# First rows of the expert weights subtracted by eight plain adding DMAs with repeated source rows, in place of sixteen gathers

## The reference

```
xn = _layernorm(x, axis=-1)
x = x + attn(xn) + ffn(xn)
attn: k, v, r = xn @ W.T;  wkv = scan over time of exp-weighted v;  out = (sigmoid(r) * wkv) @ out_w.T
ffn:  scores = softmax(xn @ gate_w.T + gate_b);  top 2 of 8 experts
      expert e: h = silu(xt @ w1e.T + b1e) * (xt @ w3e.T + b3e);  y = h @ w2e.T + b2e
      y = sum over the chosen experts of gate * y_e;  plus one shared expert of width 512
```

## Time and profile before

| | |
|---|---|
| runs of the kernel | 493.45 us median of 3 (492.17 to 494.56) |
| the profiled execution's own time | 489.11 us |
| its span, first to last instruction | 487.4 us |
| PE busy | 435.8 us (89%) |
| POOL busy | 265.7 us (55%) |
| DMA software queue q0 | 8816 packets, 21.93 MB, 17.4% of 16 engines |
| DMA hardware queue q1 | 37388 packets, 55.85 MB, 33.5% of 16 engines |

### The profile page before, as it was taken

The page is one execution under the profiler, slowest core; times in us unless marked ns, Lnnn a source line. Parts: engine busy times, 40 slices in busy tenths (PEclk is TensorE's granted clock), DMA queues, the critical chain, the costliest instruction groups (busy, mean ns, idle before and its releaser), DMA issues.

```text
span 487.4 us, 8291 instructions
## 1 busy us (share of the span) xinstructions
PE 435.8 (89%) x2522; PEld 367.0 (75%) x2522; DVE 382.1 (78%) x707; ACT 227.1 (47%) x365; POOL 265.7 (55%) x237
## 2 busy tenths in 40 slices
PE   0896064989999999999999998999999999999997
PEld 0442053778988889888888776989898989898987
DVE  7896996876788698886966478897887969696953
ACT  1445342675876858678485543141323242414131
POOL 5005988746285865859846587837262645445000
PEclk9999555799999999999999998999999999999999
DMA  5879994326567485342454692352626170705001
GB/s 177 259 253 279 304 236 97 96 80 197 209 228 250 120 270 182 133 169 91 154 144 168 213 346 69 113 200 87 195 76 206 36 244 21 258 2 174 11 33 45
DMA packets 46242, 78.27 MB, mean 161 GB/s; under 512 B 5788, under 2 KB 32132, under 8 KB 46204
## 3 DMA queue, kind: packets, MB, share of 16 engines
q1 hardware_dynamic: 37388, 55.85, 33.5%
q0 software_dynamic: 8816, 21.93, 17.4%
HBM read 49.55 MB, written 28.21 MB: 160 GB/s over the span
## 4 chain that ended last, share of the span: by engine, by line
PE 69%; DVE 8%; POOL 8%; issue 6%; DMA 5%; SPq 1%; ACT 1%; POOLq 0%; DVEq 0%; ACTq 0%
PE ps_g L971 15%; PE ps_y L971 7%; PE ps_w L1429 6%; PE ps_w L1431 5%; PE ps_w L1430 5%; PE ps_w L1495 5%; PE ps_w L1496 5%; PE ps_w L1494 5%; DMA w_lo<-w_all 4%; POOL xg L893 3%; PE ps_x L965 3%; PE ps_h L991 2%; POOL w_lo L367 2%; PE ps_v L1429 1%; PE ps_v L1431 1%
## 5 line engine op out<-in xcount | busy, mean ns | idle before, releaser
L893 POOL DMA_INDIRECT xg<-xn_rows,tile_tok x71 | 72.4, 1020 | 30.0 <-issue 17.1
L1398 POOL DMA_INDIRECT yg<-expert_rows,rows x64 | 66.2, 1034 | 23.6 <-issue 17.1
L971 PE MATMUL ps_g<-w_hi,x_hi 128*128 x142 | 57.3, 404 | 2.3 <-DVE w_lo L380 1.7
L971 PE MATMUL ps_g<-w_lo,x_hi 128*128 x142 | 57.0, 402 | 0.0
L971 PE MATMUL ps_g<-w_hi,x_lo 128*128 x142 | 56.8, 400 | 0.0
L1429 PE MATMUL ps_w<-col_hi,s_hi 128*128 128x512 f32 x128 | 50.4, 393 | 0.2 <-DVE shid L1641 0.2
L1431 PE MATMUL ps_w<-col_hi,s_lo 128*128 128x512 f32 x128 | 50.1, 392 | 0.0
L1430 PE MATMUL ps_w<-col_lo,s_hi 128*128 128x512 f32 x128 | 50.1, 392 | 0.0
L1536 ACT ACTIVATE sact<-ps_w,vec_b 128x512 f32<-128x512 f32 x32 | 22.0, 687 | 57.5 <-PE ps_w L1431 57.5
L1406 POOL TENSOR_TENSOR col_lo<-col,col_hi 128x1024 fp32r<-128x1024 f32 x7 | 20.0, 2861 | 49.8 <-ACT col_hi L1518 49.8
L1134 DVE TENSOR_TENSOR hid<-ps_g,act 128x512 f32<-128x512 f32 (+1 forms) x36 | 23.7, 660 | 26.4 <-ACT act L1046 26.2
(11 more groups left out here) (214 smaller groups left out, 1261.6 us busy)
## 6 DMA issues: line engine op xcount, KB each, us to landing
expert_rows<-y SPq DMA_DIRECT2D x35, 256.0 KB, 2.3
w_lo<-w_all SPq DMA_DIRECT2D x16, 384.0 KB, 11.6
table<-mix_tables SPq DMA_DIRECT2D x8, 768.0 KB, 7.5
xin<-x SPq DMA_DIRECT2D x16, 256.0 KB, 3.0
xn_rows<-xn SPq DMA_DIRECT2D x16, 256.0 KB, 3.4
xn_columns<-xT SPq DMA_DIRECT2D x8, 512.0 KB, 3.7
col<-xn_columns SPq DMA_DIRECT2D x8, 512.0 KB, 6.0
res<-x SPq DMA_DIRECT2D x16, 256.0 KB, 3.5
```

What stands on the lines that cost most here:

```text
L893: pool.indirect_dma_start(out=xg[b][:, t, :], out_offset=None, in_=xn_d[:, :], in_offset=bass.IndirectOffsetOnAxis(ap=tile_tok[:, 2 * a + ...
L971: mm = nc.tensor.matmul(out, x[:, k, :], w[:, ds(e, 1), k, cols].rearrange("p o n -> p (o n)"), start=(k == 0 and n == 0), stop=(last and ...
L1398: pool.indirect_dma_start(out=yg[a.buf(2)][:, k, q, :], out_offset=None, in_=y_d[:, :], in_offset=bass.IndirectOffsetOnAxis(ap=picked[a.bu ...
```

## The change

`first_rows` has only the eight negated rows. For each pair of experts (2 x pair, 2 x pair + 1) and each half k there is one plain DMA with an addition, eight in all, n = 2 x pair + k. Its source is the two experts' rows, repeated for every partition by a step of zero. For k = 0 it covers 128 partitions; for k = 1 it covers 127, which leaves the bias alone. It waits for both parts that it touches, 4 x pair + k and 4 x pair + 2 + k. `split_hi` waits for the DMA that covers its part. The tables `row_of1`, `lane`, `row` and `off127`, the zeroing of `w_neg` and the waits for these are gone.

```diff
-        def less_first(pool, i):
-            e, k = divmod(i, KC)
-            index = lane_i[:, e:e + 1] if k == 0 else row_of1[:, e:e + 1]
-            pool.wait_ge(s_w[i], 16)
+        def less_first(pool, n):
+            pair, k = divmod(n, KC)
+            rows = P - k
+            for e in (2 * pair, 2 * pair + 1):
+                pool.wait_ge(s_w[e * KC + k], 16)
             pool.sem_inc(s_lgo, 1)
-            pool.indirect_dma_start(
-                out=w_parts[1][:, i, 0:2 * FF].bitcast(F32), out_offset=None, in_=nw_d,
-                in_offset=bass.IndirectOffsetOnAxis(ap=index, axis=0), compute_op=ALU.add
-            ).then_inc(s_less[i], 16)
+            pool.dma_start(w_lo[0:rows, 2 * pair:2 * pair + 2, k, 0:2 * FF].bitcast(F32),
+                           nw_d[None, 2 * pair:2 * pair + 2, :].broadcast_to([rows, 2, 2 * FF]), accum_op=ALU.add
+                           ).then_inc(s_less[n], 16)
 
         def split_hi(act, i):
-            act.wait_ge(s_less[i], 16)
+            act.wait_ge(s_less[i // 4 * KC + i % KC], 16)
...
-            nc.gpsimd.memset(w_neg[:], 0.0).then_inc(s_negz, 1)
...
-            nc.gpsimd.iota(row_i[:], pattern=[[0, 1]], base=0, channel_multiplier=1).then_inc(s_const, 1)
...
-            pool.wait_ge(s_row1, 1)
             pool.wait_ge(s_xn, NSTEP - 1)
-            for i in range(8):
-                less_first(pool, i)
+            for n in range(E // 4 * KC):
+                less_first(pool, n)
...
-            for i in range(8, E * KC):
-                less_first(pool, i)
+            for n in range(E // 4 * KC, E // 2 * KC):
+                less_first(pool, n)
...
-            nc.vector.tensor_copy(lane[:], lane_i[:]).then_inc(s_lane, 1)
             nc.vector.tensor_copy(lane_b[:], lane_i[:, :, None].broadcast_to([P, P, BATCH]))
             nc.vector.tensor_copy(tok_b[:], tok_i[:])
-            nc.vector.tensor_copy(row[:], row_i[:]).then_inc(s_lane, 1)
             nc.vector.tensor_copy(desc[:], desc_i[:])
-            dve.wait_ge(s_lane, 2)
-            nc.vector.tensor_scalar(off127[:], row[:], float(P - 1), float(E), ALU.is_ge, ALU.mult
-                                    ).then_inc(s_off, 1)
-            dve.wait_ge(s_off, 1)
-            nc.vector.tensor_scalar(row_of1[:], lane[:, 0:E], off127[:], None, ALU.add).then_inc(s_row1, 1)
```

More of the change, by code:

```diff
@@ L135, in build @@
     tab_d = nc.dram_tensor("mix_tables", (T // PIECE, P, 3, KC, PIECE), F32, kind="Internal").ap()
-    nw_d = nc.dram_tensor("first_rows", (2 * E, 2 * FF), F32, kind="Internal").ap()
+    nw_d = nc.dram_tensor("first_rows", (E, 2 * FF), F32, kind="Internal").ap()
     y_d = nc.dram_tensor("expert_rows", (TILES * P, C), F32, kind="Internal").ap()
@@ L161, in build @@
             lane_i = sb("lane_i", [P, P], I32, experts, "right")
-            row_of1 = sb("row_of1", [P, E], I32, experts, "right")
             route_sync, route_gpsimd, route_tensor, route_scalar, route_vector, placed = route(
                 nc, kept, x, first, decay, vec_tf, vec_td, gate_w, gate_b, w_all, w_first, nw_d, xn_d, xT_d, ident, slots, gates,
-                  tile_tok, tile_exp, w_hi, w_lo, terms, lane_i, row_of1)
+                  tile_tok, tile_exp, w_hi, w_lo, terms, lane_i)
             raw_s13 = sb("raw_s13", [P, KC, 2 * SF], F32)
@@ L226, in route @@
 def route(nc, kept, x, first, decay, vec_tf, vec_td, gate_w, gate_b, w_all, w_first, nw_d, xn_d, xT_d, ident, slots, gates,
-          tile_tok, tile_exp, w_hi, w_lo, terms, lane_i, row_of1):
+          tile_tok, tile_exp, w_hi, w_lo, terms, lane_i):
     with ExitStack() as ctx:
@@ L254, in route @@
         gb = sb("gb", [E, 1], F32)
-        w_neg = sb("w_neg", [2 * E, 2 * FF], F32)
-        off127 = sb("off127", [P, 1], F32)
+        w_neg = sb("w_neg", [E, 2 * FF], F32)
         ones_f = sb("ones_f", [P, P], F32)
@@ L262, in route @@
         before = sb("before", [P, P], BF16)
-        lane = sb("lane", [P, P], F32)
         desc_i = sb("desc_i", [P, E], I32)
@@ L297, in route @@
         tok_i = sb("tok_i", [P, NT], I32)
-        row_i = sb("row_i", [P, 1], I32)
-        row = sb("row", [P, 1], F32)
         tok_f = sb("tok_f", [P, TILES], F32)
@@ L314, in route @@
         s_w = [sem(f"s_w{i}") for i in range(E * KC)]
-        s_less = [sem(f"s_less{i}") for i in range(E * KC)]
-        s_negz = sem("s_negz")
+        s_less = [sem(f"s_less{n}") for n in range(E // 2 * KC)]
         s_negl = sem("s_negl")
@@ L319, in route @@
         s_negd = sem("s_negd")
-        s_lane = sem("s_lane")
-        s_off = sem("s_off")
-        s_row1 = sem("s_row1")
         s_lgo = sem("s_lgo")
@@ L402, in sync @@
                 if i == 1:
-                    sp.wait_ge(s_negz, 1)
-                    sp.dma_start(w_neg[0:E, :], w_first).then_inc(s_negl, 16)
+                    sp.dma_start(w_neg[:], w_first).then_inc(s_negl, 16)
             def step(a):
@@ L498, in scalar @@
             act.wait_ge(s_small, 64)
-            act.wait_ge(s_const, 8)
+            act.wait_ge(s_const, 7)
             for i in range(NSTEP - 1):
@@ L542, in back @@
                 mm.then_inc(s_LT, 1)
-            pe.wait_ge(s_const, 6)
+            pe.wait_ge(s_const, 5)
             pe.wait_ge(s_small, 64)
@@ L569, in vector @@
         def vector(dve):
-            dve.wait_ge(s_const, 6)
-            nc.vector.tensor_copy(lane[:], lane_i[:]).then_inc(s_lane, 1)
+            dve.wait_ge(s_const, 5)
             nc.vector.tensor_copy(lane_b[:], lane_i[:, :, None].broadcast_to([P, P, BATCH]))
             nc.vector.tensor_copy(tok_b[:], tok_i[:])
-            nc.vector.tensor_copy(row[:], row_i[:]).then_inc(s_lane, 1)
             nc.vector.tensor_copy(desc[:], desc_i[:])
-            dve.wait_ge(s_lane, 2)
-            nc.vector.tensor_scalar(off127[:], row[:], float(P - 1), float(E), ALU.is_ge, ALU.mult
-                                    ).then_inc(s_off, 1)
-            dve.wait_ge(s_off, 1)
-            nc.vector.tensor_scalar(row_of1[:], lane[:, 0:E], off127[:], None, ALU.add).then_inc(s_row1, 1)
             nc.vector.tensor_copy(ones[:], ones_f[:])
```

## The result

The changed kernel takes 655.7 us, median of 4 runs (653.77 to 657.43); the kernel before, run beside it, 492.88 us, median of 4 (492.17 to 494.56). That is 1.327 times as long, 95% interval 1.322 to 1.332. The forecast was slower at 530 us, range 489 to 548: the direction came true, the size was missed by 126 us. The profiled execution took 653.77 us, its span is 651.9 us, at a mean granted clock of 0.840.

What follows compares the result with a forecast made beforehand. PE bounds from about 95 us on, so only the moment of its first tokens counts: 118.9 us against 82.44, +36.5. 489.11 + 36.5 = 525.6 us, 530 us against the median; own range 516 to 548, carried down to 489.

Steps and rivals of the forecast that it cites:

- One engine for 254 rows: Each 127-partition DMA on POOL's queue puts all 254 rows on one DMA engine: 45.7 us instead of 2.9 spread.
- Different engines for the long ones: The four 127-partition DMAs each go to another DMA engine; this case was given 0.76.
- The earlier long ones don't add: n = 1, 3 and 5 start 7 to 22 us sooner on other engines, done at about 95 to 112 us.
- The sum for one long DMA: n = 7 from last load to landing: 67.8 + 2.8 + 2.9 + 45.7 = 119.2 us, less 0.8: 118.4.
- POOL's own work for a long DMA: POOL's time to write a DMA's 254 rows, with 3.8 us instead of 1.5 for its longest gather in the upper bound.
- The gathers of tokens behind n = 7: Token gathers queue behind n = 7 on its engine, none completing sooner; 0.5 us added, first tokens at 118.9 us.
- ACT's wait of some 50 us: Sign of being right: ACT waits some 50 us in all for subtractions at its splits.
- DVE's start, -0.8 us: Four DVE instructions and a POOL memset go, so all of routing moves 0.8 us forward; ends 0.4 and 2.9 us.
- The slack at part 0: n = 0 also waits for part 2, so ACT's split of part 0 has 1 us of slack instead of 3.6.
- rival 1: All 127-partition DMAs are spread over the engines and nothing is slower: -1.9 us, 491.5 us against the median; chance 0.17.
- After PE's first turn nothing changes: Everything from PE's first turn on keeps its length, with the granted clock at 0.5 when it begins.
- Rival 2: All four long DMAs go to one engine, one behind the other: +158 us, about 655 us; chance 0.07.

Runs made afterwards that it cites:

- e3: Changed kernel with each k = 1 DMA taking one expert, 127 partitions with one row each, eight instead of four: 489.95 us, 0.9905 of before.
- e5: Changed kernel with the k = 1 DMAs covering 61 partitions instead of 127, 122 rows each: 507.06 us, one run.
- e11: Changed kernel with the k = 1 DMAs covering 113 partitions instead of 127, 226 rows each: 551.89 us, one run.
- e10: Changed kernel with n = 1 and 3 cut in 112 and 15 partitions, n = 5 and 7 left whole: 565.01 us, one run.
- e9: Changed kernel with n = 1, 3 and 5 cut in 112 and 15 partitions, only n = 7 left whole: 526.18 us, one run.
- e6: Changed kernel with the k = 1 DMAs covering 31 partitions instead of 127, 62 rows each: 487.83 us, one run.
- e1: Changed kernel with all eight DMAs on 128 partitions, so the bias rows are changed too: 491.51 us, 0.9905 of before.
- e8: Changed kernel with sixteen plain adding DMAs, one per part, one row per partition, with the gathers' waits: 483.43 us, 0.9899 of before.
- e12: Kernel before, gathers kept, without the second list, its DVE instructions, the memset of w_neg and the iota: 494.46 us, 1.0013 of before.

## Why the prediction was wrong, point by point

**One engine for 254 rows: right.** It was drawn from 13 completions in SP's queue. The traffic of 80 to 90 us shows it on POOL's own queue, one row every 0.158 us. The reason given, that 127 is a prime, is only half of it: e3 shows that the second count in the DMA matters as well. By the prediction's rule e3 would have been slow too.

**Different engines for the long ones: right.** e5 (three engines at once) and e11 (two) show it. In the changed kernel itself no two long ones overlap, so there it can't be seen.

**"The earlier long ones don't add": this step failed.** The prediction says: "n = 1 (issued when part 3 is in, 46.04 us, rows 4), n = 3 and n = 5 start some 7 to 22 us sooner, each on another engine, and are done at about 95 to 112 us". It put different engines to mean side by side, and took for granted that POOL can issue as soon as the loads are in. n = 1 did land at 97.4. But n = 3 was not issued until then, nor n = 5 until 147.6, nor n = 7 until 197.9. The working with the measured pieces: 43.55 + 53.8 (n = 1, with loads' packets in between) + 3 x 50.1 = 247.7 us, against 118.4 for the last landing. The same addition gives 57.4 + 2 x 50.1 = 157.6 for e10 (measured 158.28 at PE) and 68.7 + 49.8 = 118.5 for e9 (119.29). Each 254-row DMA beyond the first adds 39 to 50 us, however many engines are free.

**The sum for one long DMA: right by errors that cancel.** Its price of a row, 0.18 us, is how long a packet lasts; rows follow each other every 0.158 us, so 254 of them take 40.1 us and not 45.7. Against that stand 2.8 us from issue to the first row and 2.9 us for n = 6 ahead of it, where e9 has 9.7 us over the rows: 7.0 of POOL's writing, before which nothing moves, and 2.7 of the rest. So 51.4 us from issue to landing was said and 49.8 measured. The issue itself was put at 67.0 us and came at 68.74. Both misses are small beside the failed step, but the agreement to 1 us doesn't confirm the terms.

**Why POOL stands still.** What fits all runs is a limit on entries that wait in each engine's part of the software queue, counted alike on all 16. A DMA takes as many entries on every engine as on the fullest: 254 + 1 for 127 partitions, 16 + 1 for 128, 122 + 1 for 61, 226 + 1 for 113. That it takes them on idle engines too is seen in the packets. The page counts 20,909 packets under 512 B against 5,788 before, 15,121 more; 4 DMAs x 15 other engines x 254 = 15,240, less the 128 completions of eight DMAs fewer, is 15,112. The trace has exactly 15,240 packets of 8 bytes, in four bursts of 3,810. From 104 to 106 us, when POOL has just written n = 3, the other engines work off the first of a burst, 473 small packets with four rows between them:

```profile
DMA packets 477, 0.01 MB, mean 6 GB/s; under 512 B 473, under 2 KB 473, under 8 KB 477
```

Which DMA was let in and which was not, entries that were waiting plus its own:

| | let in | held |
|---|---|---|
| e6, all eight, at most | 4 x 63 + 4 x 17 = 320 | |
| e5, n = 6, then n = 7 | 3 x 123 + 3 x 17 = 420 | 543 |
| e11, n = 4, then n = 5 | 2 x 227 + 2 x 17 = 488 | 715 |
| e10, n = 6, then n = 7 | 255 + 17 = 272 | 527 |
| after, n = 2, then n = 3 | 255 + 17 = 272 | 527 |

The limit lies between 488 and 527 entries by this count, an estimate. Room comes only when the oldest is done, even on engines that have long worked off their share: the first burst is over at 61.6 us and n = 3 is held until 97.64. POOL goes on within 0.3 us of ACT, so of the landing, in the changed kernel, e5, e10 and e11. Two other limits don't fit. One on DMAs under way: e5 has six, where the changed kernel is held with two. One on rows of all engines together: in e1 n = 3 is issued at 48.28 us, before n = 0 lands at 51.1, which makes 4 x 256 = 1024 rows, where the changed kernel is held at 764. The runs show the pattern and the bounds; that it is this bookkeeping inside the queue is inferred, not seen.

**POOL's own work for a long DMA: too small.** Priced at 1.5 to 3.8 us, it is 6.99 (2.3 us with 62 rows, 3.8 with 122, 1.2 with 256 rows over 16 engines). It grows with the rows on the one engine, as it would if the small packets for the other 15 were written too; that they are its cost is inferred. The forecast's range had it as a few us in its upper bound.

**The gathers of tokens behind n = 7: right.** The second, issued at 206.64 us, lands 41.79 us later and lets PE begin; in e9 PE stood idle 41.5 us for it. The 128-partition DMAs behind a long one land after 42 to 53 us, also as foreseen.

**ACT's wait of some 50 us** was 189.2 us, by the same failed step.

**DVE's start, -0.8 us:** measured -1.0. The slack at part 0 was used up: n = 0 landed at 51.9 us where rival 1 had put it at 49.7, and DVE waited 0.71 us; the work list was 1.73 us sooner all the same.

**After PE's first turn nothing changes: right to 1.5 us,** 403.4 against 404.9, and the granted clock at 0.5, the 1.2 GHz level, when it begins.

**The rivals.** Rival 2 gave 655 us and got the time by luck, with a mechanism that e5 and e11 speak against: one engine for all four. It had been given 0.07 since such a choice would be odd; what was missing was a third way to put the long ones one behind the other, through the engine that issues them. Rival 1, spread, is what e1 to e3 and e8 do: 0.990 to 0.994 against the -1.9 us, 0.996, that was priced.

**What stays open.** The forms that work gain about 1%, 5 us for e8 in its comparison, while PE's first turn comes 3.0 us sooner in a trace from another chip. From that turn to the end the traces of the forms that aren't slow differ by more than the gap, 402.4 us in e8 and 409.1 in e1 against 404.9 before, so traces of different chips can't divide the gain. e12 shows that the start alone gives nothing that can be measured, at most 0.2%; what it gives once POOL no longer holds back the gathers wasn't run. That POOL's first gather of tokens begins 3.0 us sooner in e8 is shown; the rest isn't assigned. For the one-engine form only primes were run (127, 113, 61, 31).

## What to carry to other kernels

Before a software DMA goes in, look at its count of partitions: if it is a prime like 127 and a second count follows, cut it (112 + 15) or give it one row for each partition, measure other counts that 16 doesn't divide, and look in the profile for one engine's share (7.1% here, since packets overlap) and for extra packets under 512 B. "Other engines are free" doesn't mean side by side: ask whether the issuing engine is free as well: here POOL stood still until the older long DMA had landed, and with it all that stood behind, the token gathers too. And when a rival hits the number, check its mechanism before believing it; one run with one long DMA and one with two told the two stories apart.

## What the runs showed of the hardware that was not expected

- POOL's issue stops for up to 45.8 us, shown as "issue" and not as a wait, when a second DMA of 254 rows on one engine is to be issued before the first has landed.
- A DMA on one engine puts a small packet for each of its rows on each of the other 15, 15,240 in all, and takes POOL 7.0 us instead of 1.2. Rows of n = 7 go only once POOL has written all of it, the first 1.0 us after that; in e9 too none goes before.
- 127 partitions are spread with one row each (11.4 us to landing) and not with two (49.8 us).
- Rows of 2 KB added in place go every 0.158 us on one DMA engine that works alone, and 6.4 in 1 us on each when all 16 are at work. A packet lasts 0.178 us, longer than the spacing, so one busy engine shows a share of 7.1% and 16 show 114%.
